# Linear attention in a decoder: TensorE's products in another order, moments a period later, norms and gates on ScalarE

## The reference

```python
def flow_attention(x):                        # x: [32, 100, 256]
    q = sigmoid(heads(x @ Wq.T + bq)); k = sigmoid(heads(x @ Wk.T + bk)); v = heads(x @ Wv.T + bv)
    sink_in  = 1 / einsum('nhld,nhd->nhl', q + EPS, k.sum(axis=2) + EPS)
    src_out  = 1 / einsum('nhld,nhd->nhl', k + EPS, q.sum(axis=2) + EPS)
    sink     = einsum('nhld,nhd->nhl', q + EPS, (k * src_out[..., None]).sum(axis=2) + EPS)
    source   = clip(einsum('nhld,nhd->nhl', k + EPS, (q * sink_in[..., None]).sum(axis=2) + EPS), -1, 1)
    kv  = einsum('nhld,nhlm->nhdm', k, v * (softmax(source) * L)[..., None])
    out = einsum('nhld,nhdm->nhlm', q * sink_in[..., None], kv) * sigmoid(sink)[..., None]
    return merge(out) @ Wo.T + bo
x3 = layernorm(x_plus_shared + sum of the 6 chosen experts' rows, weighted)
x4 = layernorm(x3 + flow_attention(x3))
```

## Time and profile before

| | |
|---|---|
| median of 3 runs | 2705.04 us (2704.58 to 2707.52) |
| the profiled execution | 2707.99 us |
| its span, first to last instruction | 2706.20 us |
| busy in the span | PE 2240.3 us (83%), DVE 1623.5 (60%), ACT 931.0 (34%), POOL 1042.3 (39%) |
| `linear_attention` in the span | first gather at 1257.9 us, last norm (L1757) at 1685.2 us |
| mean granted clock of TensorE | 0.842 |

### The profile page before, as it was taken

One profiled execution on the slowest core, in us unless ns is written; L12 is line 12 of the kernel. 1 busy time (PEld: TensorE's weight loads), 2 busy tenths in 40 slices (PEclk: granted clock), 3 DMA queues, 4 the chain that ended last, 5 costly groups with the idle time before them and its releaser, 6 DMA issues. The chain is left out here.

```text
span 2706.2 us, 58559 instructions
## 1 busy us (share of the span) xinstructions
PE 2240.3 (83%) x20660; PEld 1706.4 (63%) x20660; DVE 1623.5 (60%) x3760; ACT 931.0 (34%) x1877; POOL 1042.3 (39%) x1026
## 2 busy tenths in 40 slices
PE   6999978999969994994688877599999999995476
PEld 4666656887857783773677776366666666663233
DVE  1444431223247773332566664489999999983898
ACT  1444433333311110341111111144444444442697
POOL 0111111231207776003766650155555555552233
PEclk9999988998967776997777667699999999996555
DMA  2001016222121111996332220201001000001111
GB/s 63 27 28 31 27 46 227 91 92 62 49 57 39 38 39 22 297 317 202 72 74 72 69 58 13 67 29 31 30 30 30 30 29 29 28 15 45 48 58 45
DMA packets 179947, 179.73 MB, mean 66 GB/s; under 512 B 47121, under 2 KB 168094, under 8 KB 178848
## 3 DMA queue, kind: packets, MB, share of 16 engines
q1 hardware_dynamic: 155295, 157.68, 18.7%
q0 software_dynamic: 24576, 21.07, 3.6%
HBM read 140.70 MB, written 56.25 MB: 73 GB/s over the span
## 5 line engine op out<-in xcount | busy, mean ns | idle before, releaser
L2275 ACT ACTIVATE xa_prob<-xa_A 121x1600 f32<-121x1600 f32 x96 | 144.5, 1506 | 304.0 <-PE xa_A L2155 304.0
L2345 POOL TENSOR_TENSOR xa_prob<-xa_prob,xa_exp_bias 121x1600 f32<-121x1600 f32 x64 | 228.5, 3571 | 41.0 <-ACT xa_prob L2275 41.0
L1094 POOL DMA_INDIRECT slot_rows<-rt_x_again,rt_slot_u x192 | 195.3, 1017 | 118.2 <-DVE rt_w_keep L1183 62.2
L2445 DVE TENSOR_REDUCE xa_kq<-xa_A 100x4 f32<-100x1444 f32 x128 | 211.6, 1653 | 20.8 <-PE xa_A L2128 20.6
L1456 POOL DMA_INDIRECT la_rows<-slot_out,la_ids x192 | 200.2, 1043 | 57.9 <-issue 55.5
L2425 DVE TENSOR_SCALAR xa_rows_n<-xa_rows_t,xa_mv,xa_rstd 121x256 f32<-121x256 f32 x128 | 142.4, 1171 | 2.4 <-POOL xa_rstd L2362 2.4
L871 DVE TENSOR_REDUCE xs_smax<-xs_B 100x8 f32<-100x360 f32 x32 | 17.1, 533 | 191.8 <-PE xs_B L767 191.8
L2155 PEld LDWEIGHTS xa_A<-xa_q2T,xa_kqT 17*121 17x121 f32 x3072 | 93.9, 185 | 56.5 <-DVE xa_kq L2445 35.9
L2128 PE MATMUL xa_A<-xa_kqT 16*100 16x361 f32 x1024 | 112.8, 509 | 10.0 <-ACT xa_prob L2275 6.9
L2155 PE MATMUL xa_A<-xa_q2T,xa_kqT 17*121 17x100 f32 x3072 | 109.4, 280 | 13.8 <-DVE xa_kq L2445 13.2
L568 DVE TENSOR_REDUCE sa_kq<-sa_A 100x16 f32<-100x1600 f32 x32 | 58.5, 1827 | 102.8 <-PE sa_A L329 102.8
(11 more groups left out here) (331 smaller groups left out, 5608.1 us busy)
## 6 DMA issues: line engine op xcount, KB each, us to landing
ex_w<-in_w13T SPq DMA_DIRECT2D x64, 352.0 KB, 4.6
xs_ctxT<-in_ctxT SPq DMA_DIRECT2D x32, 512.0 KB
xa_rows_t<-in_ctx SPq DMA_DIRECT2D x96, 121.0 KB
ex_w<-in_w2T SPq DMA_DIRECT2D x64, 176.0 KB
slot_rows<-xs_zero SPq DMA_DIRECT2D x8, 1024.0 KB
ex_x_t<-slot_rows SPq DMA_DIRECT2D x64, 128.0 KB, 2.6
slot_out<-ex_y SPq DMA_DIRECT2D x64, 128.0 KB, 5.0
sa_x_t<-in_x_tokens SPq DMA_DIRECT2D x32, 100.0 KB
```

What stands on the lines that cost most here:

```text
L1094: nc.gpsimd.indirect_dma_start(slot_rows, bass.IndirectOffsetOnAxis(slot_u[:, u, k:k + 1], 0), x_again[:, u, :], None, bounds_check=SLOTS - 1,
L2275: nc.scalar.activation(prob[:, n, :].rearrange("p (h a) -> p h a", h=HPG), A[:ROWS, :, 0:G * T], ACT.Exp, scale=EXP_SCALE).then_inc(exp_re ...
L2345: nc.gpsimd.tensor_tensor(chunk, chunk, exp_bias[:, n, :].unsqueeze(1).to_broadcast([ROWS, HEADS, T]), ALU.mult).then_inc(biased, 1)
L2445: nc.vector.tensor_reduce(kq[:T, k, NCH, 4 * j:4 * j + 4, DH:DH + 1].rearrange("p h o -> p (h o)"), A[:T, :, 0:src_len], axis=AXIS_X, op=A ...
```

## The change

In TensorE's period, `conserved(b)` moves ahead of `turn_rows(b+1)`, both behind `attend(b-1)`, and `project(b+1)` behind `turn_y(b-1)`; `values(b+1)` goes behind `project_out(b-1)`. `project_out` gets two more products, a row of ones by the row `bo`, which add the bias in PSUM; `add_bias` and `x_bo` go, and ScalarE's `keep` copies the normed x to `x_keep` for `residual`. The moments go from the end of VectorE's period to the head of the next one. The two norms become ScalarE activations, rstd * x + shift with shift = -mean * rstd; GpSimd makes `nmean` and `shift` around its root, behind two of the twelve gathers. `qk` is made by ScalarE ahead of `qke`. VectorE's additions are spread in other portions, and `residual` and `first_weights` come before `bias_values`.

```diff
@@ -1440,53 +1444,48 @@
 
             @block.gpsimd
             def _(pool):
-                pool.sem_inc(xbo_ready, LEAD)
-                pool.sem_inc(rstd_ready, LEAD - 2)
+                for sem in (nmean_ready, rstd_ready, shift_ready):
+                    pool.sem_inc(sem, LEAD - 2)
+                nc.gpsimd.memset(one_row[:], 1.0)
                 nc.gpsimd.memset(ones[:], 1.0).then_inc(ones_set, 1)
+                nc.gpsimd.memset(minus[:], -1.0)
                 nc.gpsimd.memset(power[:], -0.5).then_inc(power_set, 1)
                 pool.wait_ge(power_set, 1)
 
-                def gather(b, two):
-                    k = b[1] % 2
-                    if two == 0:
+                def gather(b, first, last):
+                    k = b[1] % 2
+                    if first == 0:
                         pool.wait_ge(ids_loaded[k], loads_of(b, 1))
                         pool.wait_ge(added, at(later(b, -2), 2 * TOPK, 2 * TOPK))
                         pool.sem_inc(ids_seen, 1)
-                    for n in range(TOPK):
-                        nc.gpsimd.indirect_dma_start(rows[:, k, two, n, :], None, slot_out,
-                                                     bass.IndirectOffsetOnAxis(ids[:, k, two, n:n + 1], 0)).then_inc(gathered[k], 16)
+                    for n in range(first, last):
+                        two, e = divmod(n, TOPK)
+                        nc.gpsimd.indirect_dma_start(rows[:, k, two, e, :], None, slot_out,
+                                                     bass.IndirectOffsetOnAxis(ids[:, k, two, e:e + 1], 0)).then_inc(gathered[k], 16)
 
                 def roots(b, has):
                     four = slice(0 if has(2) else 2, 4 if has(-1) else 2)
                     pool.wait_ge(var_ready, at(b, 1, 1))
+                    pool.wait_ge(shift_ready, at(later(b, -1), 1, 1))
+                    nc.gpsimd.tensor_tensor(nmean[:, four], mv[:, four, 0], minus[:, four], ALU.mult).then_inc(nmean_ready, 1)
                     if has(1):
                         pool.wait_ge(x3_ready, at(later(b, 1), 1, 1))
                     if has(-2):
                         pool.wait_ge(out_ready, at(later(b, -2), 1, 1))
                     nc.gpsimd.tensor_tensor(rstd[:, four], var[:, four], power[:, four], ALU.pow).then_inc(rstd_ready, 1)
-
-                def add_bias(b):
-                    k = b[1] % 2
-                    pool.wait_ge(x3_ready, at(b, 1, 1))
-                    pool.wait_ge(r_ready, at(later(b, -2), 1, 1))
-                    nc.gpsimd.tensor_tensor(x_bo[:, k], x_3[:, k], bo[:].unsqueeze(1).to_broadcast([T, 2, D]), ALU.add).then_inc(xbo_ready, 1)
+                    pool.wait_ge(nmean_ready, at(b, 1, 1))
+                    pool.wait_ge(rstd_ready, at(b, 1, 1))
+                    nc.gpsimd.tensor_tensor(shift[:, four], nmean[:, four], rstd[:, four], ALU.mult).then_inc(shift_ready, 1)
 
                 def body(b, has):
+                    if has(3):
+                        gather(later(b, 3), 0, 2)
                     if has(1) or has(-2):
                         roots(later(b, -1), lambda d: has(d - 1))
                     if has(3):
-                        gather(later(b, 3), 0)
-                    if has(0):
-                        add_bias(b)
-                    if has(3):
-                        gather(later(b, 3), 1)
-
-                def begin(b, has):
-                    if b[1] == 0:
-                        pool.wait_ge(w_in, W_ALL)
-                    body(b, has)
-
-                periods(pool, NU, FIRST, LAST, REACH, begin)
+                        gather(later(b, 3), 2, 2 * TOPK)
+
+                periods(pool, NU, FIRST, LAST, REACH, body)
 
             @block.tensor
             def _(pe):
@@ -1600,8 +1599,9 @@
                     pe.wait_ge(yT_ready, at(b, 1, 1))
                     for two in range(2):
                         for c in range(KC):
-                            last = nc.tensor.matmul(X[7][:T, two * D:(two + 1) * D], yT[:, c, two * T:(two + 1) * T], wo[:, c, :],
-                                                    start=(c == 0), stop=(c == KC - 1))
+                            nc.tensor.matmul(X[7][:T, two * D:(two + 1) * D], yT[:, c, two * T:(two + 1) * T], wo[:, c, :],
+                                             start=(c == 0), stop=False)
+                        last = nc.tensor.matmul(X[7][:T, two * D:(two + 1) * D], one_row[:], bo[:], start=False, stop=True)
                     last.then_inc(o_done, 1)
 
                 def body(b, has):
@@ -1609,25 +1609,24 @@
                         denominators(b)
                     if has(-1):
                         keys_values(later(b, -1))
-                    if has(1):
-                        turn_rows(later(b, 1))
                     if has(0):
                         weighted_sums(b)
                     if has(-1):
                         attend(later(b, -1))
+                    if has(0):
+                        conserved(b)
                     if has(1):
-                        project(later(b, 1))
-                    if has(0):
-                        conserved(b)
+                        turn_rows(later(b, 1))
                     if has(-1):
                         turn_y(later(b, -1))
                     if has(1):
-                        values(later(b, 1))
+                        project(later(b, 1))
                     if has(0):
                         sum_exponentials(b)
                     if has(-1):
                         project_out(later(b, -1))
                     if has(1):
+                        values(later(b, 1))
                         turn_qk(later(b, 1), 0)
                         turn_qk(later(b, 1), 1)
 
@@ -1635,9 +1634,35 @@
 
             @block.scalar
             def _(act):
-                for sem, per in ((xT_ready, 1), (th_ready, 2 * KC), (qke_ready, 1), (tok_ready, 2), (ecs_ready, 1), (yT_ready, 1)):
+                for sem, per in ((x3_ready, 1), (kept, 1), (xT_ready, 1), (th_ready, 2 * KC), (qk_ready, 1), (qke_ready, 1), (tok_ready, 2), (ecs_ready, 1),
+                                 (yT_ready, 1), (out_ready, 1)):
                     act.sem_inc(sem, per * LEAD)
                 act.wait_ge(half_set, 1)
+
+                def normalise(b):
+                    k = b[1] % 2
+                    act.wait_ge(shift_ready, at(later(b, -2), 1, 1))
+                    act.wait_ge(x_turned, at(later(b, -2), 1, 1))
+                    act.wait_ge(kept, at(later(b, -2), 1, 1))
+                    for two in range(2):
+                        last = nc.scalar.activation(x_3[:, k, two, :], acc[:, k, two, :], ACT.Identity, scale=rstd[:, two:two + 1],
+                                                    bias=shift[:, two:two + 1])
+                    last.then_inc(x3_ready, 1)
+
+                def keep(b):
+                    k = b[1] % 2
+                    act.wait_ge(x3_ready, at(b, 1, 1))
+                    act.wait_ge(r_ready, at(later(b, -2), 1, 1))
+                    nc.scalar.activation(wide(x_keep[:, k]), wide(x_3[:, k]), ACT.Copy).then_inc(kept, 1)
+
+                def finish(b):
+                    k = b[1] % 2
+                    act.wait_ge(shift_ready, at(later(b, 1), 1, 1))
+                    act.wait_ge(stored[k], 16 * (b[1] // 2) + 16 + b[0] * 16)
+                    for two in range(2):
+                        last = nc.scalar.activation(x_o[:, k, two, :], r[:, two, :], ACT.Identity, scale=rstd[:, 2 + two:3 + two],
+                                                    bias=shift[:, 2 + two:3 + two])
+                    last.then_inc(out_ready, 1)
 
                 def rows_out(b):
                     act.wait_ge(x_turned, at(b, 1, 1))
@@ -1656,6 +1681,9 @@
                     k = b[1] % 2
                     act.wait_ge(th_ready, at(b, 2 * KC, 2 * KC))
                     act.wait_ge(cons_done, at(later(b, -2), 1, 1))
+                    act.wait_ge(attended, at(later(b, -2), 1, 1))
+                    nc.scalar.activation(qk[:, k].rearrange("p j t -> p (j t)"), th[:].rearrange("p j t -> p (j t)"), ACT.Copy,
+                                         scale=0.5, bias=0.5).then_inc(qk_ready, 1)
                     nc.scalar.activation(qke[:, k].rearrange("p j t -> p (j t)"), th[:].rearrange("p j t -> p (j t)"), ACT.Copy,
                                          scale=0.5, bias=0.5 + EPS).then_inc(qke_ready, 1)
 
@@ -1735,28 +1769,9 @@
...
-                    dve.wait_ge(rstd_ready, at(later(b, -1), 1, 1))
+                    dve.wait_ge(shift_ready, at(later(b, -1), 1, 1))
...
-                def normalise(b):
...
-                def finish(b):
...
@@ -1837,54 +1852,45 @@
                     heads = v[:, k].rearrange("t two (h d) -> t (two h) d", d=DH)
                     nc.vector.tensor_tensor(heads, heads, wide(comp[:]).unsqueeze(2).to_broadcast([T, 2 * HEADS, DH]), ALU.mult).then_inc(vc_ready, 1)
 
-                def plain_gates(b):
```

(34 more changed lines are left out.)

41 lines of the change are left out of this document (18 added, 23 removed).

## The result

The changed kernel took 2720.73 us (median of 5 runs, 2715.61 to 2727.1) against 2705.04 for the one before: ratio 1.0055, 95% interval 1.0036 to 1.0074. Timed twice more beside the kernel before, it came to 1.0029 (1.0018 to 1.0039) and 1.0032 (1.0015 to 1.0049). So it is slower, by 0.3 to 0.55%, 8 to 15 us by the ratios. I had forecast 2709.5 as likeliest, 4.5 over before, with 2688 to 2718.

The account below looks back on a forecast made before the run. TensorE was taken to set linear_attention's 23.85 us period. New period 7.3 + 16.3 = 23.6, so -3 over 13 periods, head +2.3, tail +4.8: +4, kept as +4.5, giving 2709.5 us; range 2688 to 2718.

Parts of the forecast that it names:

- VectorE's part, 7.3 us: Linear_attention's new period: VectorE's chain from the end of project_out to weighted_sums, all on the path, 7.3 us.
- TensorE's part, 16.3 us: Linear_attention's new period: TensorE's work from weighted_sums through project_out, 16.3 us, including 0.89 for the bias products.
- Period 23.6: Linear_attention's new period, 7.3 + 16.3 = 23.6 us against 23.85; over 13 periods -3 us.
- rival A: Low-clock stretch of the period gets shorter: -1.7 us each, 2687.5, or 2690 to 2705 in part; chance 0.28.
- Head +2.3: Start of linear_attention: first root behind two more gathers, plus nmean, shift and slower norm, partly given back; +2.3 us.
- Tail +4.8: End of linear_attention: last two project_out biases at the lower level, 3.6, plus 1.2 in the last chain; +4.8 us.
- Only this stage can move the time: Nothing outside linear_attention changes and no other stage waits for its inner semaphores, so only it moves the time.
- the ring: Linear_attention's period as a closed chain: project_out's end through VectorE to weighted_sums, then TensorE back to project_out; 23.6 us.
- B: Clock stays up in linear_attention's periods as the wait shortens; GpSimd's 18.3 us then decides, -72 us, 2638; chance 0.04.
- C: Project starts at the lower level and the clock rises only behind it; +13 us, 2722; chance 0.13 together with D.
- D: The wait only moves: VectorE's part is 7.8 instead of 7.3; +6.5 us, 2716; chance 0.13 together with C.
- the fall precedes the wait: In the period before, the clock is low from 1419.28 and TensorE's wait for normed rows starts at 1420.16.

Follow-up runs that it names:

- e3: Changed kernel with the two bias products side by side, so two changes between 128-row and one-row products a period instead of four; 2718.45 us, ratio 1.0027.
- e6: Changed kernel with GpSimd's roots put back ahead of the first two gathers of the period; 2714.88 us, ratio 1.0021.
- e7: On top of e1, all weighted additions of a period done before the competition, while TensorE projects; 2646.05 us, ratio 0.9774 to the kernel before.
- e1: Changed kernel with the bias added by GpSimd where it makes x_keep, instead of by products on TensorE; 2697.14 us, ratio 0.9953 to the kernel before.
- e2: Kernel before plus only two products in project_out, a row of zeros by the bias row; 2711.02 us, ratio 1.0008.

## Why the prediction missed

The direction and most steps stood. Point by point:

- **VectorE's part, 7.3 us:** 6.99. The wait moved ahead of weighted_sums and is 1.8 us, as forecast (1.6 to 2.1).
- **TensorE's part, 16.3 us:** 17.23. This is the step that failed, by its term for the bias: 0.89 forecast, 1.47 measured (3.26 - 1.79). I took half of project_out, as the columns are the same. But each pair takes 0.60 from start to start, and each four before it 1.02 to 1.04 for 0.89: beside the columns there is a cost for going from 128 rows to one and back. e3 removes two of the four changes and 0.27 us, so all four are worth about 0.54 of the 0.58 that I had missed. The rest of the 0.93 is 0.11 in weighted_sums, 0.16 in turn_y, 0.07 in project.
- **Period 23.6:** 23.91 in the mean; the one walked above is 24.2. Four of the stage's fifteen low stretches were 10.2 us, rival A in a part of the periods, which gave back some of the bias: 0.9 us in such a period, where A had 1.7. Between the second and the last reciprocal I expected -3 and got -0.3.
- **Head +2.3:** +3.35. To the first reciprocal it is 5.7: the first root itself took 1.30 beside the running work for 0.74, behind the two gathers I had counted (e6: 2.2 us). The next period gave back 2.4, of the 0 to 2.7 I allowed.
- **Tail +4.8:** +4.46, and its closeness is luck. Project_out with its bias takes 6.12 us at the lower level (1671.42 to 1677.54) for 3.41 before, so its two products cost 2.7, over the 1.79 that I had called the ceiling; with the last one the bias is 5.3 rather than 3.6. The other way, the last weighted_sums fell into the upper level, 1.82 us for 3.28, and about 0.5 of the norm's 1.2 showed.
- **"Only this stage can move the time":** true of the cause, not of a measurement. Stages with unchanged code differ by up to 8 us from profile to profile, and the first profile carried 6 of them. The stage's own +8 is what the two later comparisons show (+0.29% and +0.32%, 8 to 9 us); beside them the forecast of +4.5 is off by the ring's 3 and the head's 1.
- **Rivals.** B did not come. C did not: the rise is 3.4 us behind project's start (mean of ten) as before, and project takes 4.47. D has the right size for the wrong reason. Against the Trainium skill (TensorE: Matmul & The Clock Gate, "HAM oscillation — how this bites in real kernels"), which lays the fall to idle gaps between bursts, I held that the fall precedes the wait, and took the wait to be innocent of it. e7 speaks against that: with the wait taken away the fall came 1.9 us later and the stretches lost 3.4 to 6.9 us. The Trainium skill's account is nearer to the runs there than mine, though it does not explain why e7, with 0.3 us of wait a period, still falls in every one.

What the change gains and loses, by the square: new order and moments, without the bias products, -0.47% (e1, -12 us); bias products in it, +0.78%; norms and gates on ScalarE, nothing. What it left undone was the lever: 1.66 us of additions on VectorE's part of the ring, worth 1.8% once the bias products are off it (e7).

## What to carry to other kernels

When an order is changed, write down the new ring first, and then ask of each piece of work on it whether it must be there: the additions could go elsewhere for nothing and were worth some 49 us with the bias off TensorE, and the bias products, nearly free in the old order, cost 21 in the new, half of it because the new order had put o_done on the ring. Price a product by its row in the trace only if its shape is there; two one-row products among 128-row ones cost 1.65 times what their columns say. And before laying a few microseconds to a change, look at what untouched stages do from profile to profile.

## What the runs showed of the hardware

- Around a one-row product TensorE's weight load stands 0.70 us at the lower level with no releaser (0.35 at the upper), going there and coming back.
- Taking 1.9 us of wait from a period of 23.2 shortened it by 3.7 (e7 beside e1): the low stretch began later and was 3.8 us shorter. TensorE was busy 191.48 of 194.84 us in e7 and still fell to the lower level in every period.
- The low stretches came in few lengths (6.8, 10.2 or 13.7 us in most periods), so a period answers to small edits in jumps: e3 saved 0.27 us of work and next to no time. Where the difference lies over a wait, it is worth nothing: e2 has 10.2 for 13.7 us and the same period.
- On two of the chips the untouched route took 488 us for 318, with 126.5 us of idle TensorE that nothing in the profile releases.
